# A mixture-of-experts stage regrouped: 20 tiles of four 32-token blocks in place of 24 tiles of two 64-token blocks

## The chip, the cores and the metric

The kernel runs on one core of one Trainium2 chip. The metric is the device time of one execution in microseconds (us), of which the profile covers the span from the first to the last instruction. A core has TensorE (PE; its weight loads are shown as PEld), VectorE (DVE), ScalarE (ACT), GpSimd (POOL) and SyncE (SP), each with its own instruction stream. They meet at semaphores. An engine name with a q behind it is that engine's sequencer, which runs register and branch instructions and hands the others to the engine.

## The reference

16 sequences of 128 tokens with 192 features go through an embedding stage, one attention block and a Switch mixture of 16 experts:

```python
h = tok_embeddings(...)                                  # gathers, time features, layer norm
h = h + attention(_layernorm(h), ...)                    # 12 heads of 16
...
probs = softmax(normed @ w_router); expert_idx = argmax(probs)
keep = onehot * (cumsum(onehot, axis=1) <= 64)           # at most 64 tokens per sequence and expert
expert_in = einsum('bsec,bsd->becd', dispatch, normed)
hidden = relu(einsum('becd,edf->becf', expert_in, wi))   # 192 -> 768
expert_out = einsum('becf,efd->becd', hidden, wo)        # 768 -> 192
h = h + (x + router_prob * where(routed, combined, normed))
```

So each token meets one expert's `wi` (192x768) and `wo` (768x192), in float32.

## The kernel before

The kernel does embeddings and attention for eight pairs of sequences, stores one row per token to DRAM, and writes each token's number into the list of its expert. Then comes the expert stage, which is what the change is about.

Each expert's list is cut into blocks of `BT` = 64 tokens, the last one padded. With 2048 tokens and 16 experts that can be 48 blocks, so the stage always runs `NTILE` = 24 tiles of two blocks. Which expert a block belongs to depends on the data: VectorE works it out in 21 small steps, the plan (`planned(...)`, L1158 to L1213), which leaves in `blk_col` the column at which each block's expert begins in the big `weights` tile. All 16 experts are kept there; they are loaded during the attention stage by SP's queue, the last of them under conditions written out in that queue (L341 to L349).

Per tile q, five engines work in a chain of semaphores, each in the order of its own code:

- GpSimd fetches the tile's 128 token numbers (`list_tile`, L507), then the 128 rows (`gather_rows`, L515, up to three tiles ahead), and at the end scatters the results (`scatter`, L522).
- VectorE reads the two blocks' columns from `blk_col` into registers (`columns`, L1189, one `value_load` for each block), copies both experts' `wi` and later `wo` from there into `w_now` (`take_weights`, L1185, each copy 128x1152), because TensorE cannot address by a register here. `w_now` has two buffers. It also scales and adds the output (`result`, L1195 for the index, L1199 for the rows).
- TensorE transposes the rows (L1459, L1460), multiplies by `wi` (`hidden`, L1467 with 128 rows of the array, L1472 with 64), transposes the hidden layer (L1479) and multiplies by `wo` (`output`, L1488). The two blocks use the two column halves of the array side by side.
- ScalarE copies the transposed rows (L708), applies relu (L712) and copies the transposed hidden layer (L716).

TensorE's order is `turn_rows(q+1)`, `turn_hid(q)`, `hidden(q+1)`, `output(q)`. VectorE's order in the loop is

```python
for q in range(NTILE):
    if q + 1 < NTILE:
        at = columns(q + 1)
        take_weights(q + 1, 0)
    if q >= 1:
        result(q - 1)
    if q + 1 < NTILE:
        take_weights(q + 1, 1)
```

`take_weights(q, part)` waits until the tile that last used the buffer is through (`b_hid` after the hidden matmuls, `b_y` after the output matmuls): with two buffers that is tile q-2.

Of the kernel before, what the change touches and what calls it, by code (L numbers as in the profile page):

```python
# [17 lines left out]
ALU = mybir.AluOpType  # L18
# [16 lines left out]
SLOTS = NSEQ * CAP  # L35
BT = P // 2
SPLIT = SLOTS // BT
# [12 lines left out]

NBLK = NSEQ * P // BT + NE
NTILE = NBLK // 2
ROW = 2 * D + 1
# [13 lines left out]
def tower_kernel(nc, t, out):  # L67
    assert NBLK == 48 and NTILE == 24
    ctx = ExitStack()
    with ctx:  # L70
# [62 lines left out]
        rank_a, rank_b, rank_c = (share_a(8 * NE).rearrange("p (n e) -> p n e", e=NE) for _ in range(3))  # L133
        chosen = share_a(2 * P)[:, 0:8 * NE // 2].bitcast(BF16).rearrange("p (n e) -> p n e", e=NE)
# [133 lines left out]
        LG = 0  # L268
        RANK_STEPS = 12

        block = ctx.enter_context(nc.Block())
# [3 lines left out]
        def _(sp):  # L275
# [81 lines left out]
        def _(pool):  # L357
# [18 lines left out]
                           allow_small_or_imprecise_dtypes=True).then_inc(sem("ident"), 1)  # L376
            nc.gpsimd.iota(blk_idx[:, :], [[2, NTILE]], base=0, channel_multiplier=0,
                           allow_small_or_imprecise_dtypes=True).then_inc(sem("ident"), 1)
# [73 lines left out]
            def enlist(n):  # L452

                if n == 0:
                    pool.wait_ge(sem("lists0"), 16)
                    pool.wait_ge(sem("halves"), 4)
# [89 lines left out]
        def _(act):  # L546
# [179 lines left out]
            act.wait_ge(sem("rows_last"), 32)  # L726
            act.wait_ge(sem("out_last"), 32)
            turn_rows(0)
# [10 lines left out]
        def _(dve):  # L739
# [79 lines left out]
            def constants():  # L819
                dve.wait_ge(sem("vectors"), 16)  # L820
                dve.wait_ge(sem("ident"), 8)
                V.tensor_scalar(low_half[:, :], token_iota[:, 0:1], float(BT), None, ALU.is_ge).then_inc(sem("halves"), 1)
                dve.wait_ge(sem("halves"), 1)
# [322 lines left out]
            dve.wait_ge(sem("bases"), NSEQ + 1)  # L1146
            dve.wait_ge(sem("halves"), 4)
# [4 lines left out]
            over_k = shared[:, 5632:5632 + NE * SPLIT].rearrange("p (e k) -> p e k", k=SPLIT)  # L1152

# [22 lines left out]

            def take_weights(q, part):
# [4 lines left out]
                for e in range(max(2 * q, ARENA_FIRST), min(2 * q + 2, NE)):  # L1182
                    dve.wait_ge(sem(f"weights{e}"), 80)
                for k in range(2):
                    V.tensor_copy(w_now[q % 2][k][:, lo:hi], weights[:, bass.ds(at[k] + lo, hi - lo)]).then_inc(  # L1185
                        sem(("wi_now", "wo_now")[part]), 1)
# [16 lines left out]
            dve.wait_ge(sem("weights"), 80 * ARENA_FIRST)  # L1203
            at = columns(0)
            take_weights(0, 0)
            planned(V.tensor_tensor(big, over(expert_iota[:, :]), ej.unsqueeze(2).broadcast_to([P, NTILE, NE]), ALU.is_equal))
# [6 lines left out]
            planned(V.tensor_scalar(blk_pen[:, :], within, BIG, None, ALU.mult))  # L1213
            take_weights(0, 1)
# [12 lines left out]
        def _(pe):  # L1227
# [234 lines left out]
            def hidden(q):  # L1462
                pe.wait_ge(sem("gT"), q + 1)
                pe.wait_ge(sem("wi_now"), 2 * q + 2)
                for b in range(2):
                    for k in range(2):
                        T.matmul(hid_ps[k * BT:(k + 1) * BT, b, :], gT[:, b * P + k * BT:b * P + (k + 1) * BT],  # L1467
                                 w_now[q % 2][k][:, b * WI2:(b + 1) * WI2], start=True, stop=False)
                for b in range(2):
                    for k in range(2):  # L1470
                        at = (1 - b) * P + k * BT
                        last = T.matmul(hid_ps[k * BT:(k + 1) * BT, b, :], gT[REST[b], at:at + BT],  # L1472
                                        w_now[q % 2][k][REST[b], FF:WI_COLS], start=False, stop=True)
                last.then_inc(sem("b_hid"), 1)
# [7 lines left out]
            def output(q):  # L1482
                pe.wait_ge(sem("hidT"), q + 1)
                pe.wait_ge(sem("wo_now"), 2 * q + 2)
                freed(pe, sem("res"), q - 1)
                for c in range(FC):
                    for k in range(2):
                        last = T.matmul(psum[q % 2][k * BT:(k + 1) * BT, 3, 0:D], hidT[:, c * P + k * BT:c * P + (k + 1) * BT],  # L1488
                                        w_now[q % 2][k][:, WI_COLS + c * D:WI_COLS + (c + 1) * D], start=c == 0, stop=c == FC - 1)
                last.then_inc(sem("b_y"), 1)  # L1490
# [64 lines left out]
```

## Time and profile before

| | |
|---|---|
| median of 3 runs | 388.18 us (387.72 to 389.49) |
| the profiled execution's own time | 388.62 us |
| its span | 386.9 us |
| TensorE busy | 337.5 us, 87% |
| VectorE busy | 258.0 us, 67% |
| ScalarE busy | 160.9 us, 42% |
| GpSimd busy | 198.4 us, 51% |
| mean granted TensorE clock | 0.901 of full speed |

The profile is of one execution. 1.7 us of its time lie outside the span. Busy time counts an engine's own instructions, not those of its sequencer, so time in which a sequencer reads a register shows only as a gap that is put down to "issue". The shares are means over the embedding, attention and expert stages; the expert stage lies from about 236 us to the end.

### The profile page before, as it was taken

What the parts mean: (1) busy time and instruction counts of PE and PEld (TensorE: products, weight loads), DVE (VectorE), ACT (ScalarE), POOL (GpSimd) and SP (SyncE); (2) the same over time, 40 slices, a digit from 0 to 9 for tenths busy, and PEclk for the clock granted to TensorE, in tenths of its full rate; (3) what the DMA queues carried; (4) which work ended last, traced back from release to release, by engine and by line L of the source; (5) the groups of instructions that cost most, each with busy time, mean ns of one, the idle gap of its engine ahead of it and who ended that gap; (6) DMA issues with size and microseconds to landing.
All of it is one profiled execution on the core that took longest, in us unless ns stands there. A gap on an engine that the chain in (4) does not pass through costs nothing.

```text
span 386.9 us, 8606 instructions
## 1 busy us (share of the span) xinstructions
PE 337.5 (87%) x3170; PEld 217.8 (56%) x3170; DVE 258.0 (67%) x742; ACT 160.9 (42%) x299; POOL 198.4 (51%) x191
## 2 busy tenths in 40 slices
PE   8989679689899999989999724799999999999980
PEld 3435446556677776667777412265556655566550
DVE  7774937864779799996767677745666556655520
ACT  3634334514366665647556320233433334333320
POOL 5776374585268661037101255645765676666421
PEclk9566968955999999999999986899999999999995
DMA  4438921113627873371424390494222211122100
GB/s 91 108 86 224 238 66 44 45 34 50 189 32 160 229 146 90 113 195 55 135 65 122 114 255 0 112 278 129 54 57 54 61 57 35 58 55 60 30 2 0
DMA packets 35066, 37.96 MB, mean 98 GB/s; under 512 B 6214, under 2 KB 32531, under 8 KB 35022
## 3 DMA queue, kind: packets, MB, share of 16 engines
q1 hardware_dynamic: 25680, 24.20, 21.7%
q0 software_dynamic: 8768, 12.63, 15.0%
q10 hardware_dynamic: 576, 0.59, 0.5%
q8 instruction: 25, 0.41, 0.4%
q14 instruction: 17, 0.14, 0.1%
HBM read 30.97 MB, written 7.21 MB: 99 GB/s over the span
## 4 chain that ended last, share of the span: by engine, by line
PE 60%; DVE 20%; issue 7%; POOL 4%; ACT 3%; DMA 2%; POOLq 0%; DVEq 0%; ACTq 0%
PE psum L1488 13%; PE psum L1467 9%; PE psum L1238 6%; PE psum L1239 5%; PE psum L1472 5%; PE psum L1479 4%; PE psum L1294 4%; PE psum L1308 4%; POOL weights L392 2%; DVE small L835 2%; PE psum L1459 2%; PE psum L1374 2%; PE psum L1232 1%; DMA weights<-pair_rows,ids 1%; DVE weights L794 1%
## 5 line engine op out<-in xcount | busy, mean ns | idle before, releaser
L1185 DVE COPY shared<-weights 128x1152 f32 x96 | 69.7, 769 | 10.9 <-issue 10.2
L522 POOL DMA_INDIRECT tower_out<-shared,oidx x24 | 36.2, 1507 | 37.3 <-DVE shared L1199 34.7
L1488 PE MATMUL psum<-shared 128*64 128x192 f32 x576 | 52.1, 330 | 0.9 <-ACT shared L716 0.9
L1488 PEld LDWEIGHTS psum<-shared 128*64 128x64 f32 x576 | 39.2, 137 | 19.4 <-issue 13.8
L1199 DVE SCALAR_TENSOR_TENSOR shared<-psum,shared 128x192 f32<-128x192 f32 x24 | 10.0, 418 | 47.1 <-PE psum L1488 47.1
L1467 PE MATMUL psum<-shared 128*64 128x384 f32 x192 | 36.8, 505 | 0.5 <-ACT shared L708 0.5
L1238 PE MATMUL psum<-shared,weights 96*128 96x192 f32 (+1 forms) x96 | 36.0, 460 | 0.7 <-ACT weights L574 0.7
L916 DVE TENSOR_REDUCE guard<-psum 128x12 bf16<-128x1536 f32 x16 | 28.1, 1754 | 10.9 <-PE psum L1294 10.9
L712 ACT ACTIVATE shared<-psum 128x768 f32<-128x768 f32 x24 | 19.5, 812 | 37.6 <-PE psum L1472 37.6
L431 POOL TENSOR_TENSOR small<-small,mhalf 128x2 f32<-128x2 f32 x16 | 12.3, 771 | 44.1 <-DVE small L843 44.0
L1239 PE MATMUL psum<-shared,weights 97*128 97x192 f32 (+1 forms) x96 | 33.0, 428 | 0.0
L515 POOL DMA_INDIRECT shared<-token_rows,blk_token x24 | 26.1, 1086 | 11.0 <-issue 6.4
L708 ACT COPY shared<-psum 128x256 f32<-128x256 f32 x24 | 8.9, 372 | 52.6 <-PE psum L1460 52.6
L507 POOL DMA_INDIRECT blk_token<-expert_lists,blk_entry x24 | 23.7, 990 | 9.8 <-issue 7.0
L450 POOL TENSOR_TENSOR small<-small,mhalf 128x4 f32<-128x4 f32 x8 | 8.7, 1084 | 37.7 <-DVE small L955 37.7
L458 POOL DMA_INDIRECT expert_lists<-tokens,slot_i x16 | 15.8, 987 | 18.6 <-DVE slot_i L1042 14.5
L608 ACT ACTIVATE shared<-psum 128x1536 f32<-128x1536 f32 x16 | 23.2, 1448 | 3.7 <-PE psum L1317 3.6
L1239 PEld LDWEIGHTS psum<-shared,weights 97*128 97x128 f32 x96 | 19.8, 215 | 6.0 <-issue 3.0
L716 ACT COPY shared<-psum 128x768 f32<-128x768 f32 x24 | 19.2, 800 | 9.0 <-PE psum L1479 9.0
L880 DVE TENSOR_REDUCE ms_qk<-weights 128x24 f32<-128x408 f32 x16 | 9.2, 577 | 20.5 <-ACT weights L579 20.5
L579 ACT ACTIVATE weights<-psum 128x384 f32<-128x384 f32 x16 | 7.9, 491 | 34.7 <-PE psum L1239 34.7
L1472 PE MATMUL psum<-shared 64*64 64x384 f32 x192 | 21.7, 523 | 0.0
(196 smaller groups left out, 714.8 us busy)
## 6 DMA issues: line engine op xcount, KB each, us to landing
weights<-in_wo SPq DMA_DIRECT2D x16, 576.0 KB, 6.9
weights<-in_wi SPq DMA_DIRECT2D x32, 192.0 KB, 4.8
weights<-in_wi SPq DMA_DIRECT2D x32, 96.0 KB, 5.2
token_rows<-shared SPq DMA_DIRECT2D x14, 192.5 KB
tower_out<-shared SPq DMA_DIRECT2D x14, 96.0 KB
token_rows<-shared ACTq DMA_DIRECT2D x2, 192.5 KB, 3.0
blk_token<-expert_lists,blk_entry POOLq DMA_INDIRECT x24, 2.5
shared<-token_rows,blk_token POOLq DMA_INDIRECT x24, 3.3
```

Source lines behind the costliest of these rows:

```text
L507: G.indirect_dma_start(out=blk_token[:, q:q + 1], out_offset=None, in_=lists, in_offset=bass.IndirectOffsetOnAxis(ap=blk_entry[:, q:q + 1] ...
L515: G.indirect_dma_start(out=grow[q % 4], out_offset=None, in_=rows, in_offset=bass.IndirectOffsetOnAxis(ap=blk_token[:, q:q + 1], axis=0),) ...
L522: G.indirect_dma_start(out=out, out_offset=bass.IndirectOffsetOnAxis(ap=oidx[q % 2][:, :], axis=0), in_=res[q % 2], in_offset=None, bounds ...
L608: S.activation(probsT[u], psum_s.rearrange("p b c -> p (b c)"), ACT.Exp).then_inc(sem(f"probs{u}"), 1)
L712: S.activation(hid.rearrange("p (b c) -> p b c", b=2), hid_ps, ACT.Relu).then_inc(sem("hid"), 1)
L916: V.tensor_reduce(guard16[u][:, :].rearrange("p (g c) -> p g c", c=HPAD)[:, :, 0:CHUNKS], psum_s.rearrange("p g (c m) -> p g c m", m=P), A ...
L1185: V.tensor_copy(w_now[q % 2][k][:, lo:hi], weights[:, bass.ds(at[k] + lo, hi - lo)]).then_inc(sem(("wi_now", "wo_now")[part]), 1)
L1238: T.matmul(dst, xt[0:HALF, 0:P], w[0:HALF, 0, start:start + width], start=True, stop=False)
L1239: return T.matmul(dst, xt[0:k1, P:2 * P], w[0:k1, 1, start:start + width], start=False, stop=True)
L1467: T.matmul(hid_ps[k * BT:(k + 1) * BT, b, :], gT[:, b * P + k * BT:b * P + (k + 1) * BT], w_now[q % 2][k][:, b * WI2:(b + 1) * WI2], start ...
L1472: last = T.matmul(hid_ps[k * BT:(k + 1) * BT, b, :], gT[REST[b], at:at + BT], w_now[q % 2][k][REST[b], FF:WI_COLS], start=False, stop=True)
L1488: last = T.matmul(psum[q % 2][k * BT:(k + 1) * BT, 3, 0:D], hidT[:, c * P + k * BT:c * P + (k + 1) * BT], w_now[q % 2][k][:, WI_COLS + c * ...
```

## The change

Blocks have 32 tokens instead of 64 (`NB` = 4, `BT` = 32). That makes at most 80 blocks, in 20 tiles of four; a tile still has 128 tokens. The four blocks use the four column quarters of the array. Four experts' weights fill the room that the two buffers of two had, so `w_now` has one buffer: the copies for tile q wait for `hidden(q-1)` and `output(q-1)`. VectorE copies three of the four experts and reads three columns; ScalarE copies the fourth and reads its column (`take_last`, `last_column`), and for the first tile it waits for the end of the whole plan. In VectorE's loop the copies of `wo` for tile q come after those of `wi` for tile q+1, and `result(q-1)` comes last. In SP's queue expert 12 is loaded together with 10 and 11, and the last two no longer wait for the row gather of tile 2 (`rows2`). The plan's arrays and two constants are sized anew.

```diff
-BT = P // 2
+NB = 4
+BT = P // NB
...
-        w_now = [[share_b(WCOL) for _ in range(2)] for _ in range(2)]
+        w_now = [share_b(WCOL) for _ in range(NB)]
...
-            for e in (10, 11):
+            for e in (10, 11, 12):
                 load_expert(e)
             sp.wait_ge(sem("p_logit0"), NPAIR)
             sp.wait_ge(sem("p_logit1"), NPAIR)
-            sp.wait_ge(sem("rows2"), 16)
-            for e in (12, NE - 2, NE - 1):
-                load_expert(e)
+            load_expert(NE - 2)
+            load_expert(NE - 1)
...
+            def take_last(q, part):
+                lo, hi = ((0, WI_COLS), (WI_COLS, WCOL))[part]
+                freed(act, sem(("b_hid", "b_y")[part]), q)
...
+                S.copy(w_now[NB - 1][:, lo:hi], weights[:, bass.ds(last_at[q % 2] + lo, hi - lo)]).then_inc(
+                    sem(("wi_last", "wo_last")[part]), 1)
...
+            act.wait_ge(sem("plan"), N_PLAN)
+            last_at = [last_column(0), None]
+            take_last(0, 0)
+            take_last(0, 1)
             turn_rows(0)
             relu(0)
             for q in range(NTILE):
                 if q + 1 < NTILE:
+                    last_at[(q + 1) % 2] = last_column(q + 1)
+                    take_last(q + 1, 0)
                     turn_rows(q + 1)
                 turn_hid(q)
+                if q >= 1:
+                    take_last(q, 1)
                 if q + 1 < NTILE:
                     relu(q + 1)
...
-                if q >= 2:
-                    dve.wait_ge(sem(("b_hid", "b_y")[part]), q - 1)
+                freed(dve, sem(("b_hid", "b_y")[part]), q)
...
-                return [dve.value_load(blk_col[k * BT:k * BT + 1, q:q + 1], min_val=0, max_val=(NE - 1) * WCOL) for k in range(2)]
+                return [dve.value_load(blk_col[k * BT:k * BT + 1, q:q + 1], min_val=0, max_val=(NE - 1) * WCOL) for k in range(NB - 1)]
...
             for q in range(NTILE):
                 if q + 1 < NTILE:
-                    at = columns(q + 1)
-                    take_weights(q + 1, 0)
+                    at[(q + 1) % 2] = columns(q + 1)
+                    take_weights(q + 1, 0, (0, 1, 2))
                 if q >= 1:
+                    take_weights(q, 1, (0, 1, 2))
                     result(q - 1)
-                if q + 1 < NTILE:
-                    take_weights(q + 1, 1)
             result(NTILE - 1)
```

What this does to the order is seen best in VectorE's stream. Before, one tile in the middle of the stage reads as follows (L1195 and L1199 are `result`, TENSOR_LOAD with its two ISA rows is one `value_load`, a COPY with the ISA row ahead of it is one copy of weights; the piece ends with the first of two `wi` copies):

```order
L1195 TENSOR_TENSOR oidx<-blk_token,blk_pen 128x1 [waits s_scattered1,s_blk_token1]
L1199 SCALAR_TENSOR_TENSOR shared<-psum,shared 128x192 [waits s_oidx,s_b_y]
L1185 ISA [waits s_b_y]
L1185 COPY shared<-weights 128x1152
L1185 ISA
L1185 COPY shared<-weights 128x1152
L1189 TENSOR_LOAD blk_col
L1189 ISA x2
L1189 TENSOR_LOAD blk_col
L1189 ISA x2
L1185 ISA [waits s_b_hid]
L1185 COPY shared<-weights 128x1152
```

Of the changed kernel the same stretch of VectorE's stream, from `result` (now L1221 and L1225) to the first of three `wi` copies (L1211):

```order
L1221 TENSOR_TENSOR oidx<-blk_token,blk_pen 128x1 [waits s_scattered1,s_blk_token1]
L1225 SCALAR_TENSOR_TENSOR shared<-psum,shared 128x192 [waits s_oidx,s_b_y]
L1215 TENSOR_LOAD blk_col
L1215 ISA x2
L1215 TENSOR_LOAD blk_col
L1215 ISA x2
L1215 TENSOR_LOAD blk_col
L1215 ISA x2
L1211 ISA [waits s_b_hid]
L1211 COPY shared<-weights 128x1152
```

The two `wo` copies that stood between `result` and the register loads are gone from there; three loads follow the row instruction at once, and all six copies follow the loads.

On ScalarE the entry into the stage read, before (row copy and relu of tile 0, then row copy, hidden copy and relu of the loop):

```order
L708 COPY shared<-psum 128x256 [waits s_b_gT,s_out_last,s_rows_last]
L712 ACTIVATE shared<-psum 128x768 [waits s_b_hid]
L708 COPY shared<-psum 128x256 [waits s_b_gT]
L716 COPY shared<-psum 128x768 [waits s_b_hidT]
L712 ACTIVATE shared<-psum 128x768 [waits s_b_hid]
```

and in the changed kernel (L740 is `last_column`, L736 the copy of weights, L710, L714 and L718 what L708, L712 and L716 were):

```order
L740 TENSOR_LOAD blk_col [waits s_weights,s_blk_entry,s_plan,s_out_last,s_rows_last]
L740 ISA x2
L736 ISA
L736 COPY shared<-weights 128x1152
L736 ISA
L736 COPY shared<-weights 128x1152
L710 COPY shared<-psum 128x256 [waits s_b_gT]
L714 ACTIVATE shared<-psum 128x768 [waits s_b_hid]
L740 TENSOR_LOAD blk_col
L740 ISA x2
L736 ISA [waits s_b_hid]
L736 COPY shared<-weights 128x1152
```

A load and two copies, behind the plan's end, now stand ahead of the row copy of tile 0; in the loop a load and a copy stand between relu and the next row copy.

## Rows read from the trace of the kernel before

**Rows 1.** Busy time of each engine in three stretches, with granted clock and DMA.

```profile
core 0: us, PE busy (x) PEld busy (x) DVE busy (x) ACT busy (x) POOL busy (x), PEclk, DMA share, GB/s
...
215.00:220.00 5.00, 3.68 (x39) 2.06 (x40) 3.88 (x17) 1.16 (x3) 0.00 (x0) 1.00 0.37 123
225.00:230.00 5.00, 0.71 (x7) 0.54 (x6) 3.59 (x21) 1.67 (x6) 3.23 (x4) 0.83 0.97 269
270.00:370.00 100.00, 100.00 (x894) 58.86 (x888) 60.94 (x112) 36.89 (x56) 65.38 (x54) 1.00 0.19 50
```

**Rows 2.** TensorE in order of time, one tile of the steady stage.

```profile
302.77 0.82 PE L1479 MATMUL psum<-ident,shared 128*128 128x128 f32 x6
303.52 1.51 PE L1467 MATMUL psum<-shared 128*64 128x384 f32 x8
...
305.77 2.17 PE L1488 MATMUL psum<-shared 128*64 128x192 f32 x24
307.87 0.33 PE L1459 MATMUL psum<-ident,shared 128*128 128x128 f32 x1
```

**Rows 3.** VectorE in order of time, the same tile.

```profile
302.62 0.42 DVE L1199 SCALAR_TENSOR_TENSOR shared<-psum,shared 128x192 f32<-128x192 f32 x1 [1.80 <-PE psum L1488]
302.95 1.42 DVE L1185 COPY shared<-weights 128x1152 f32 x2
304.71 1.44 DVE L1185 COPY shared<-weights 128x1152 f32 x2 [0.34 <-issue]
306.07 0.14 DVE L1195 TENSOR_TENSOR oidx<-blk_token,blk_pen 128x1 int32<-128x1 int32 x1
307.99 0.42 DVE L1199 SCALAR_TENSOR_TENSOR shared<-psum,shared 128x192 f32<-128x192 f32 x1 [1.78 <-PE psum L1488]
```

**Rows 4.** Instructions of line 1189 on VectorE's sequencer, 302 to 306.3 us.

```profile
L1189 DVEq TENSOR_LOAD <-blk_col x2: 528/529/530, 302.9 to 303.7; - x2
L1189 DVEq FUSED_REGOPS  x2: 190/190/190, 303.5 to 304.3; - x2
```

**Rows 5.** TensorE in order of time, a matmul of the attention stage on column quarters.

```profile
135.23 0.86 PE L1334 MATMUL psum<-shared,weights 128*32 128x128 f32 x24
```

**Rows 6.** GpSimd in order of time, a scatter of the steady stage.

```profile
303.87 1.72 POOL L522 DMA_INDIRECT tower_out<-shared,oidx  x1 [1.03 <-DVE shared L1199]
```

**Rows 7.** All engines in order of time, entry into the expert stage.

```profile
236.29 0.18 DVE L1175 TENSOR_TENSOR blk_entry<-shared 128x24 int32<-128x24 f32 x1
...
238.37 1.43 DVE L1185 COPY shared<-weights 128x1152 f32 x2 [1.90 <-issue]
...
240.30 0.95 POOL L515 DMA_INDIRECT shared<-token_rows,blk_token  x1 [0.32 <-issue]
...
242.78 1.55 DVE L1185 COPY shared<-weights 128x1152 f32 x2 [0.16 <-DVE blk_pen L1213]
...
244.51 2.07 PE L1467 MATMUL psum<-shared 128*64 128x384 f32 x8 [0.54 <-ACT shared L708]
...
248.00 0.47 PE L1459 MATMUL psum<-ident,shared 128*128 128x128 f32 x1
```

**Rows 8.** ScalarE's groups of instructions, busy us and mean ns, whole span.

```profile
L608 ACT ACTIVATE shared<-psum 128x1536 f32<-128x1536 f32 x16 | 23.2, 1448 | 3.7 <-PE psum L1317 3.6
...
L716 ACT COPY shared<-psum 128x768 f32<-128x768 f32 x24 | 19.2, 800 | 9.0 <-PE psum L1479 9.0
...
L708 ACT COPY shared<-psum 128x256 f32<-128x256 f32 x24 | 8.9, 372 | 52.6 <-PE psum L1460 52.6
```

**Rows 9.** SP's queue in order of time, the last load of expert 11.

```profile
224.06 0.59 SPq L304 DMA_DIRECT2D weights<-in_wo  x1
```

**Rows 10.** DMA issues with median us to landing, 236 to 240 us.

```profile
blk_token<-expert_lists,blk_entry POOLq DMA_INDIRECT x2, 2.5
```

**Rows 11.** The same view, 250 to 262 us.

```profile
blk_token<-expert_lists,blk_entry POOLq DMA_INDIRECT x1, 5.9
```

**Rows 12.** All engines in order of time, the end of the kernel.

```profile
376.31 0.42 DVE L1199 SCALAR_TENSOR_TENSOR shared<-psum,shared 128x192 f32<-128x192 f32 x1 [3.38 <-PE psum L1488]
377.53 0.97 POOL L522 DMA_INDIRECT tower_out<-shared,oidx  x1 [2.89 <-DVE shared L1199]
```

More of the change, by code:

```diff
@@ L51 @@
 NBLK = NSEQ * P // BT + NE
-NTILE = NBLK // 2
+NTILE = NBLK // NB
 ROW = 2 * D + 1
@@ L67, in tower_kernel @@
 def tower_kernel(nc, t, out):
-    assert NBLK == 48 and NTILE == 24
+    assert NBLK == 80 and NTILE == 20
     ctx = ExitStack()
@@ L132, in tower_kernel @@
         bases = share_a(NSEQ * NE).rearrange("p (n e) -> p n e", e=NE)
-        rank_a, rank_b, rank_c = (share_a(8 * NE).rearrange("p (n e) -> p n e", e=NE) for _ in range(3))
+        rank_a = share_a(8 * NE).rearrange("p (n e) -> p n e", e=NE)
+        rank_b = share_a(8 * SPLIT).rearrange("p (n k) -> p n k", k=SPLIT)
         chosen = share_a(2 * P)[:, 0:8 * NE // 2].bitcast(BF16).rearrange("p (n e) -> p n e", e=NE)
@@ L269, in tower_kernel @@
         RANK_STEPS = 12
+        N_PLAN = 21
         block = ctx.enter_context(nc.Block())
@@ L376, in _ @@
                            allow_small_or_imprecise_dtypes=True).then_inc(sem("ident"), 1)
-            nc.gpsimd.iota(blk_idx[:, :], [[2, NTILE]], base=0, channel_multiplier=0,
+            nc.gpsimd.iota(blk_idx[:, :], [[NB, NTILE]], base=0, channel_multiplier=0,
                            allow_small_or_imprecise_dtypes=True).then_inc(sem("ident"), 1)
@@ L455, in enlist @@
                     pool.wait_ge(sem("lists0"), 16)
-                    pool.wait_ge(sem("halves"), 4)
+                    pool.wait_ge(sem("halves"), 6)
                 pool.wait_ge(sem("slots"), batch_of(n) + 1)
@@ L727, in _, with last_column @@
             act.wait_ge(sem("out_last"), 32)
+            def take_last(q, part):
+                lo, hi = ((0, WI_COLS), (WI_COLS, WCOL))[part]
+                freed(act, sem(("b_hid", "b_y")[part]), q)
+                for e in range(max(NB * q, ARENA_FIRST), min(NB * q + NB, NE)):
+                    act.wait_ge(sem(f"weights{e}"), 80)
+                S.copy(w_now[NB - 1][:, lo:hi], weights[:, bass.ds(last_at[q % 2] + lo, hi - lo)]).then_inc(
+                    sem(("wi_last", "wo_last")[part]), 1)
+            def last_column(q):
+                return act.value_load(blk_col[(NB - 1) * BT:(NB - 1) * BT + 1, q:q + 1], min_val=0, max_val=(NE - 1) * WCOL)
+            act.wait_ge(sem("blk_entry"), 1)
+            act.wait_ge(sem("weights"), 80 * ARENA_FIRST)
+            act.wait_ge(sem("plan"), N_PLAN)
+            last_at = [last_column(0), None]
+            take_last(0, 0)
+            take_last(0, 1)
             turn_rows(0)
@@ L822, in constants @@
                 V.tensor_scalar(low_half[:, :], token_iota[:, 0:1], float(BT), None, ALU.is_ge).then_inc(sem("halves"), 1)
-                dve.wait_ge(sem("halves"), 1)
+                for k in range(1, NB - 1):
+                    dve.wait_ge(sem("halves"), k)
+                    V.scalar_tensor_tensor(low_half[:, :], token_iota[:, 0:1], float((k + 1) * BT), low_half[:, :], ALU.is_ge, ALU.add).then_inc(sem("halves"), 1)
+                dve.wait_ge(sem("halves"), NB - 1)
                 V.scalar_tensor_tensor(half_pos[:, :], low_half[:, :], -float(BT), token_iota[:, 0:1], ALU.mult, ALU.add).then_inc(sem("halves"), 1)
@@ L1146, in _ @@
             dve.wait_ge(sem("bases"), NSEQ + 1)
-            dve.wait_ge(sem("halves"), 4)
+            dve.wait_ge(sem("halves"), 6)
             big, big2 = (shared[:, 4608 + 512 * k:4608 + 512 * k + NTILE * NE].rearrange("p (j e) -> p j e", e=NE) for k in range(2))
@@ L1151, in _ @@
             nth, ej, before, within, length, late = (cols(plan, 112 + 32 * a, NTILE) for a in range(6))
-            over_k = shared[:, 5632:5632 + NE * SPLIT].rearrange("p (e k) -> p e k", k=SPLIT)
+            over_k = shared[:, 6288:6288 + NE * SPLIT].rearrange("p (e k) -> p e k", k=SPLIT)
             def over(v):
@@ L1175, in _, with take_weights @@
             V.tensor_tensor(blk_entry[:, :], length, late, ALU.add).then_inc(sem("blk_entry"), 1)
-            def take_weights(q, part):
+            def take_weights(q, part, blocks):
                 lo, hi = ((0, WI_COLS), (WI_COLS, WCOL))[part]
-                if q >= 2:
-                    dve.wait_ge(sem(("b_hid", "b_y")[part]), q - 1)
-                for e in range(max(2 * q, ARENA_FIRST), min(2 * q + 2, NE)):
+                freed(dve, sem(("b_hid", "b_y")[part]), q)
+                for e in range(max(NB * q, ARENA_FIRST), min(NB * q + NB, NE)):
                     dve.wait_ge(sem(f"weights{e}"), 80)
-                for k in range(2):
-                    V.tensor_copy(w_now[q % 2][k][:, lo:hi], weights[:, bass.ds(at[k] + lo, hi - lo)]).then_inc(
+                for k in blocks:
+                    V.tensor_copy(w_now[k][:, lo:hi], weights[:, bass.ds(at[q % 2][k] + lo, hi - lo)]).then_inc(
                         sem(("wi_now", "wo_now")[part]), 1)
             def columns(q):
-                return [dve.value_load(blk_col[k * BT:k * BT + 1, q:q + 1], min_val=0, max_val=(NE - 1) * WCOL) for k in range(2)]
+                return [dve.value_load(blk_col[k * BT:k * BT + 1, q:q + 1], min_val=0, max_val=(NE - 1) * WCOL) for k in range(NB - 1)]
             def result(q):
@@ L1203, in _ @@
             dve.wait_ge(sem("weights"), 80 * ARENA_FIRST)
-            at = columns(0)
-            take_weights(0, 0)
+            at = [columns(0), None]
+            take_weights(0, 0, (0, 1))
             planned(V.tensor_tensor(big, over(expert_iota[:, :]), ej.unsqueeze(2).broadcast_to([P, NTILE, NE]), ALU.is_equal))
@@ L1213, in _ @@
             planned(V.tensor_scalar(blk_pen[:, :], within, BIG, None, ALU.mult))
-            take_weights(0, 1)
+            assert steps[0] == N_PLAN
+            take_weights(0, 0, (2,))
+            take_weights(0, 1, (0, 1, 2))
             for q in range(NTILE):
                 if q + 1 < NTILE:
-                    at = columns(q + 1)
-                    take_weights(q + 1, 0)
+                    at[(q + 1) % 2] = columns(q + 1)
+                    take_weights(q + 1, 0, (0, 1, 2))
                 if q >= 1:
+                    take_weights(q, 1, (0, 1, 2))
                     result(q - 1)
-                if q + 1 < NTILE:
-                    take_weights(q + 1, 1)
             result(NTILE - 1)
@@ L1463, in hidden @@
                 pe.wait_ge(sem("gT"), q + 1)
-                pe.wait_ge(sem("wi_now"), 2 * q + 2)
+                pe.wait_ge(sem("wi_now"), (NB - 1) * (q + 1))
+                pe.wait_ge(sem("wi_last"), q + 1)
                 for b in range(2):
-                    for k in range(2):
+                    for k in range(NB):
                         T.matmul(hid_ps[k * BT:(k + 1) * BT, b, :], gT[:, b * P + k * BT:b * P + (k + 1) * BT],
-                                 w_now[q % 2][k][:, b * WI2:(b + 1) * WI2], start=True, stop=False)
+                                 w_now[k][:, b * WI2:(b + 1) * WI2], start=True, stop=False)
                 for b in range(2):
-                    for k in range(2):
+                    for k in range(NB):
                         at = (1 - b) * P + k * BT
                         last = T.matmul(hid_ps[k * BT:(k + 1) * BT, b, :], gT[REST[b], at:at + BT],
-                                        w_now[q % 2][k][REST[b], FF:WI_COLS], start=False, stop=True)
+                                        w_now[k][REST[b], FF:WI_COLS], start=False, stop=True)
                 last.then_inc(sem("b_hid"), 1)
@@ L1483, in output @@
                 pe.wait_ge(sem("hidT"), q + 1)
-                pe.wait_ge(sem("wo_now"), 2 * q + 2)
+                pe.wait_ge(sem("wo_now"), (NB - 1) * (q + 1))
+                pe.wait_ge(sem("wo_last"), q + 1)
                 freed(pe, sem("res"), q - 1)
                 for c in range(FC):
-                    for k in range(2):
+                    for k in range(NB):
                         last = T.matmul(psum[q % 2][k * BT:(k + 1) * BT, 3, 0:D], hidT[:, c * P + k * BT:c * P + (k + 1) * BT],
-                                        w_now[q % 2][k][:, WI_COLS + c * D:WI_COLS + (c + 1) * D], start=c == 0, stop=c == FC - 1)
+                                        w_now[k][:, WI_COLS + c * D:WI_COLS + (c + 1) * D], start=c == 0, stop=c == FC - 1)
                 last.then_inc(sem("b_y"), 1)
```

## The prediction

> **What bounds the kernel now.** I went first to the stage that the change touches and read the busy time of each engine in it. From 270 to 370 us TensorE is busy all the time at full clock, VectorE and GpSimd some 60 to 65%, ScalarE 37% [rows 1]. Then TensorE in order of time: one group follows the other with no gap, 0.75 of hidden transposes (302.77 to 303.52), 2.25 of hidden matmuls (to 305.77), 2.10 of output matmuls (to 307.87), where the next tile's row transposes begin [rows 2]. VectorE's row instructions lie 307.99 - 302.62 = 5.37 apart [rows 3]; the 0.27 by which that is more than 5.10 are the row transposes. So the 24 tiles run at TensorE's pace, 5.37 us each.
>
> VectorE is the engine that gets more work, so its slack has to be read with care, and busy time isn't enough. Two copies take 1.42, then there is a gap of 0.34 put down to issue, then the other two, then 1.78 of waiting for TensorE [rows 3]. The gap is the end of something longer. VectorE's sequencer reads two block columns from 302.9 on: 0.53 for a load, 0.19 for the register work, 0.8 from one load to the next [rows 4], and the copy that needs them starts at 304.71. The two reads take 1.8 us, of which 1.47 lie hidden under the two copies that were handed to the engine just before.
>
> **TensorE's new work.** 20 tiles in place of 24 at an unchanged tile would take off 4 x 5.37 = 21.5 us. Each output or hidden matmul becomes two of half the columns of the array with the same moving width. Four quarters side by side do occur before: 24 instructions of 128 columns in about 0.8 us [rows 5], 3.9 columns per ns, against 24 of 192 in 2.10, 2.2 per ns, on halves [rows 2]. Twice the instructions at that rate make the output 2.36 and the other 128-row matmuls 1.58 instead of 1.44. The 64-row matmuls on quarters have no row: between no loss (0.8 a tile) and half the width lost (1.6), and I take no loss, since the same groups of 64 rows work side by side now (2.25 less 1.51 [rows 2] leaves them about half of what the 128-row ones take). So TensorE's own tile is 5.4 to 6.6 us.
>
> **VectorE's new tile.** Here is the step on which I rest the forecast. With one buffer and three experts a tile has six copies and three reads. In the new order the row instruction waits for the index instruction of the same engine, which waits behind all six copies; the sequencer stops at that wait, so it reaches the reads only when the engine has run dry. Then only the 0.42 of the row instruction covers them, no copies. The cycle, from one row instruction to the next:
> - row instruction to first read: 0.1 (between 0.05 and the 0.28 from 302.62 to 302.9, which had two copies to hand out);
> - three reads up to the first copy: 1.81 for two (302.9 to 304.71), plus 0.8: 2.6 [rows 3, 4];
> - six copies: 3 x 1.42 less two overlaps of 0.08 (306.15 - 306.07): 4.10 [rows 3];
> - the index instruction's 0.14 less its overlap, 0.06, and the wait on it, 0.1 (0.05 to 0.15).
>
> That is 6.96 us. Copies and GpSimd get in each other's way: a scatter beside copies took 1.72 [rows 6], one beside an idle VectorE 0.97 [rows 12], and a pair of copies beside a gather 1.55 instead of 1.42 [rows 7]. From 0 to 3 x 0.13 a tile; in the steady stage the copies lost nearly nothing, so I take 0.14. A tile takes 7.1 us (6.9 to 7.35). That is above TensorE's 5.4 to 6.6, so VectorE sets the pace and TensorE waits for `wi` at every tile. With its copies starting at T, `wi` is there at T+2.2, hidden is done at T+4.45, output at T+6.55, and VectorE needs none of these sooner: it waits for nobody.
>
> The Trainium skill (DMA: Bandwidth & Descriptors, Latency and other measured facts) puts a floor of about 600 ns under a tensor_load. The row shows 0.53, and the row decides; by the page's figure three reads would add 0.2 a tile, 3.6 us in all.
>
> **ScalarE** adds two copies of 1152 columns. 1536 cost 1.45 and 768 0.80, so 1152 cost 1.12 [rows 8]. Its tile becomes 2 x 1.12 + 2 x 0.80 + 0.37 = 4.2; its read runs while relu runs. Nothing of it is late at 7.1 a tile. GpSimd, at three issues of about 1 us, each held up by 0.75 at most [rows 6, 12], stays under 7.1 as well (3 x 1.72 = 5.2).
>
> **The entry.** VectorE's plan ends its first part at 236.47; one of its arrays doubles, others shrink by a sixth: 0.3 later (0 to 0.6). Two reads took 1.9 up to 238.37 [rows 7], three take 2.8, so the first copy is at 239.6 and the pair done at 241.0. The eight plan steps behind it took 2.8 (239.8 to 242.6) and now a little less: 243.6. Only then ScalarE starts: a read 1.0, two copies 2.24, the row copy 0.37 [rows 8]. Hidden of tile 0 can't start before 247.4; it started at 244.51 [rows 7].
>
> The other way into tile 0 is list and row gather. Before, SP's queue had given out its last early load at 224.06 [rows 9], and I put the end of that traffic near 231. Now three more experts of 1.18 MB (twice 192 x 768 floats) follow at once; at 269 GB/s [rows 1] they keep it busy for 13 us more, to about 244. Under such loads a list gather landed in 5.9 us instead of 2.5 [rows 10, 11]. The path has three transfers in a row (list write, list gather, row gather), so it is 0 to 8 us later and hidden of tile 0 starts between 247.4 and 252. I take 249, nearer to the lower end, because the last of the three falls behind the loads. The first hidden took 3.5 us (244.51 to 248.00) [rows 7], not 2.25, and I leave it so: done at 252.5. With one buffer only now come relu 0.8, ScalarE's copy 1.12, the row copy 0.37 and 0.2 of gaps: hidden of tile 1 runs from 255.0 to 257.25, and VectorE's copies for tile 2 start at T = 257.25.
>
> **The sum.** From there to the copies for tile 19 are 17 cycles: 17 x 7.1 = 120.7. The end: `wi` 2.2, hidden 2.25, output of tile 18 2.1, transposes 0.75, ScalarE's copy 0.9 and its share of `wo` 1.2, which now waits for output 18, output of tile 19 2.1, 0.1: 11.6. The last row instruction starts at 257.25 + 120.7 + 11.6 = 389.55 instead of 376.31 [rows 12]: 13.2 us later, and what follows is unchanged. The profiled execution's 388.62 become 401.8. The median of the runs is 0.44 lower; on it the sum is 401.4, and I say 401.5. The attention stage is left as it is; its slot steps grow by less than 0.5.
>
> **The rivals.**
> - *Fewer tiles win.* If the reads were reached in time, in the shadow of the copies as now, a VectorE tile would be 4.1 + 0.6 + 0.34 plus contention, about 5.3, and the pace TensorE's, say 5.6. Then 257.25 + 95.2 + 11.6 = 364.05: 12.3 earlier, 376 us. For it speaks that the same reads cost only 0.34 now. Against it: the order rows put them behind the instruction that waits for the engine itself. It decides at 17P = 376.31 - 268.85: below P = 6.32 us a tile the change wins. Chance 0.07, and 0.02 for an end near no change.
> - *TensorE is slower on quarters or cools down.* If nothing ran wider than two, hidden and output would double to 8.7, with the transposes 9.7 a tile: 17 x 2.6 = 44 more, 446 us. And the gaps of 1.7 a tile might lower the clock: it was 0.83 where TensorE was busy 0.71 of 5 us, but full at 3.68 of 5 [rows 1], the share to be expected here. Chance 0.03.
> - *The port.* If GpSimd held a copy up for a whole issue of 0.97 [rows 12] three times a tile, P were 9.9 and the time 449. The copies that ran beside GpSimd lost 0.13, not 0.97 [rows 7]. The Trainium skill (SBUF — State Buffer, SBUF: two separate sides) speaks for this one: it calls the port that the two share an exclusive lock, held for the whole instruction, the other one blocked. The scatter's 1.72 agrees with that for GpSimd; the pair's 1.55 does not for VectorE. Chance 0.03.
> - *The forecast, VectorE at 6.9 to 7.35 a tile*: 0.85.
>
> **The numbers.** The low end takes P = 6.9 (-3.4) and hidden at 247.4 (-1.6): 396.5. The high end takes P = 7.35 (+4.3) and hidden at 252 (+3): 409. The cases outside hold about 2 in 10. A measurement of this kernel can tell about 0.5%, 1.9 us, from no change; faster 0.07, same 0.02, slower 0.91.
>
> **What the new profile would show.** VectorE's row instruction every 7.1 us, then a gap of 2.2 put down to issue, then six copies without a gap; TensorE waiting about 1.7 a tile before its hidden matmuls, for VectorE's copy; hidden of tile 0 at about 249. If the distance is 5.6 and TensorE has no gaps, the reads were hidden and I am wrong in sign. If TensorE's matmuls take longer than 5.4 in sum, the quarters cost. If the gap ahead of the copies is 2.2 but copies are longer, it is the port.

## The result, and the profile after

The changed kernel took 398.32 us (median of 4 runs, 394.63 to 399.23), the kernel before 387.95 us beside it (4 runs, 386.11 to 389.49). The ratio is 1.0251, 95% interval 1.0171 to 1.0331 (the ratios here and below are not quotients of the medians and differ from them by up to 0.003). The profiled execution took 399.23 us with a span of 397.5; before it was 388.62 and 386.9.

VectorE in order of time, one tile of the steady stage of the changed kernel (start, duration, then what it is, and in brackets the idle time before it):

```profile
310.47 0.42 DVE L1225 SCALAR_TENSOR_TENSOR shared<-psum,shared 128x192 f32<-128x192 f32 x1
312.90 4.23 DVE L1211 COPY shared<-weights 128x1152 f32 x6 [2.02 <-issue]
317.05 0.15 DVE L1221 TENSOR_TENSOR oidx<-blk_token,blk_pen 128x1 int32<-128x1 int32 x1
317.30 0.42 DVE L1225 SCALAR_TENSOR_TENSOR shared<-psum,shared 128x192 f32<-128x192 f32 x1
```

This answers to [rows 3]. The row instructions lie 317.30 - 310.47 = 6.83 apart, where it was 5.37. In this stretch VectorE never waits for TensorE any more: the 1.78 in front of the row instruction is gone. The one gap in the cycle is 2.02 in front of the six copies, put down to "issue", where a gap of 0.34 was.

TensorE in order of time, the same tile and on to the next tile's first transpose:

```profile
315.18 1.50 PE L1495 MATMUL psum<-shared 128*32 128x384 f32 x16 [1.42 <-issue]
316.61 0.88 PE L1500 MATMUL psum<-shared 64*32 64x384 f32 x16
317.41 2.16 PE L1517 MATMUL psum<-shared 128*32 128x192 f32 x48
319.50 0.33 PE L1486 MATMUL psum<-ident,shared 128*128 128x128 f32 x1
```

Hidden takes 317.41 - 315.18 = 2.23 and output 319.50 - 317.41 = 2.09. Before it was 2.25 and 2.10 [rows 2], with half the instructions. Ahead of the hidden matmuls TensorE now stands still for 1.42 a tile. The label says "issue", but VectorE's copies say what it is: the first three of six, at 0.7 each, are through at about 312.90 + 2.1 = 315.0, and the matmuls begin at 315.18. ScalarE's copy of the fourth expert, from 311.46 on for 1.14, was through long before, at 312.60.

The register reads, line 1215, on VectorE's sequencer (count, shortest/median/longest ns, starts of the first and the last):

```profile
L1215 DVEq TENSOR_LOAD <-blk_col x3: 305/520/524, 317.3 to 318.8; - x3
L1215 DVEq FUSED_REGOPS  x3: 183/190/190, 317.9 to 319.3; - x3
```

And the wait ahead of the row instruction, line 1223, on the same sequencer (317 to 317.5 us):

```profile
L1223 DVEq EVENT_SEMAPHORE  x1: 21/21/21, 317.2 to 317.2; - x1
```

This is the wait for the index instruction, which ends at 317.05 + 0.15 = 317.2. It stands on the sequencer itself, and in this tile nothing that comes after it in VectorE's stream starts earlier. The first of the three loads starts at the same time as the row instruction, 317.3, and the last one's register work ends at 319.5. That is what fills the "issue" gap. Busy time of each engine in a stretch of the stage, with granted clock:

```profile
280.00:370.00 90.00, 70.40 (x1144) 38.99 (x1144) 61.68 (x106) 53.47 (x67) 45.83 (x40) 1.00 0.16 43
```

TensorE has gone from 100% [rows 1] to 78%, and VectorE, which sets the pace, shows only 69%: a sequencer's reads aren't in its busy time. The chain around the entry and the end, all engines in order of time:

```profile
240.86 1.39 POOL L509 DMA_INDIRECT blk_token<-expert_lists,blk_entry  x1 [5.61 <-DMA expert_lists<-tokens,slot_i]
...
244.91 2.21 ACT L736 COPY shared<-weights 128x1152 f32 x2 [16.80 <-DVE blk_pen L1239]
...
248.53 0.33 PE L1486 MATMUL psum<-ident,shared 128*128 128x128 f32 x1 [2.14 <-DMA shared<-token_rows,blk_token]
...
249.46 2.79 PE L1495 MATMUL psum<-shared 128*32 128x384 f32 x16 [0.46 <-ACT shared L710]
...
258.04 4.16 DVE L1211 COPY shared<-weights 128x1152 f32 x6 [2.61 <-PE psum L1500]
...
374.97 4.10 DVE L1211 COPY shared<-weights 128x1152 f32 x6 [2.01 <-issue]
...
384.51 3.32 PE L1517 MATMUL psum<-shared 128*32 128x192 f32 x48 [2.14 <-DVE shared L1225]
...
387.87 0.42 DVE L1225 SCALAR_TENSOR_TENSOR shared<-psum,shared 128x192 f32<-128x192 f32 x1 [3.39 <-PE psum L1517]
```

Hidden of tile 0 starts at 249.46, where it was 244.51 [rows 7]. The copies for tile 2 start at 258.04 and those for tile 19 at 374.97, so 17 cycles take 116.93, 6.88 each. The last row instruction starts at 387.87, which is 11.56 later than before [rows 12].

### The profile page after: what moved, and what is told of

Read it like the earlier page. It is cut to its first block, busy times and chain, and to the rows that moved or that the text cites. A ratio compares the mean times of both kernels' runs of the same rounds, so it can differ in the third digit from the quotient of the medians.

```text
span 397.5 us, 10011 instructions
## 1 busy us (share of the span) xinstructions
PE 318.0 (80%) x3766; PEld 202.7 (51%) x3778; DVE 273.4 (69%) x760; ACT 195.0 (49%) x327; POOL 180.5 (45%) x179
## 4 chain that ended last, share of the span: by engine, by line
PE 53%; DVE 20%; issue 13%; DMA 5%; POOL 4%; ACT 3%; DVEq 1%; POOLq 0%; ACTq 0%
PE psum L1517 11%; PE psum L1495 8%; PE psum L1265 6%; PE psum L1266 5%; PE psum L1500 4%; PE psum L1321 4%; PE psum L1335 3%; PE psum L1507 3%; POOL weights L394 2%; DMA expert_lists<-tokens,slot_i 2%; DVE small L862 2%; DMA weights<-pair_rows,ids 1%; PE psum L1401 1%; PE psum L1259 1%; PE psum L1486 1%
## 5 line engine op out<-in xcount | busy, mean ns | idle before, releaser
L1211 DVE COPY shared<-weights 128x1152 f32 x120 | 84.2, 768 | 48.9 <-issue 37.8
L736 ACT COPY shared<-weights 128x1152 f32 x40 | 45.9, 1151 | 16.9 <-DVE blk_pen L1239 16.8
L1495 PE MATMUL psum<-shared 128*32 128x384 f32 x320 | 31.2, 508 | 25.3 <-issue 24.2
L524 POOL DMA_INDIRECT tower_out<-shared,oidx x20 | 20.3, 1015 | 67.2 <-DVE shared L1225 63.8
L1517 PE MATMUL psum<-shared 128*32 128x192 f32 x960 | 44.3, 334 | 2.1 <-DVE shared L1225 2.1
L1517 PEld LDWEIGHTS psum<-shared 128*32 128x32 f32 x960 | 30.2, 112 | 20.6 <-issue 14.2
L714 ACT ACTIVATE shared<-psum 128x768 f32<-128x768 f32 x20 | 16.2, 810 | 39.3 <-PE psum L1500 39.3
L1495 PEld LDWEIGHTS psum<-shared 128*32 128x32 f32 x320 | 10.0, 111 | 36.8 <-issue 35.0
L509 POOL DMA_INDIRECT blk_token<-expert_lists,blk_entry x20 | 21.9, 1094 | 11.4 <-issue 5.8
L1321 PE MATMUL psum<-weights 32*128 32x128 f32 x384 | 20.5, 302 | 1.2 <-ACT weights L593 1.0
L1321 PEld LDWEIGHTS psum<-weights 32*128 32x128 f32 x384 | 17.4, 203 | 7.2 <-issue 4.8
```

Of the source, the lines that this page charges most:

```text
L509: G.indirect_dma_start(out=blk_token[:, q:q + 1], out_offset=None, in_=lists, in_offset=bass.IndirectOffsetOnAxis(ap=blk_entry[:, q:q + 1] ...
L524: G.indirect_dma_start(out=out, out_offset=bass.IndirectOffsetOnAxis(ap=oidx[q % 2][:, :], axis=0), in_=res[q % 2], in_offset=None, bounds ...
L736: S.copy(w_now[NB - 1][:, lo:hi], weights[:, bass.ds(last_at[q % 2] + lo, hi - lo)]).then_inc(sem(("wi_last", "wo_last")[part]), 1)
L1211: V.tensor_copy(w_now[k][:, lo:hi], weights[:, bass.ds(at[q % 2][k] + lo, hi - lo)]).then_inc(sem(("wi_now", "wo_now")[part]), 1)
L1321: last = T.matmul(psum_s[:, g, c * P:(c + 1) * P], qT[u][rows_, c * P:(c + 1) * P], kT[u][rows_, c * P:(c + 1) * P], start=True, stop=True)
```

## The experiments

The theory was that the three reads stand bare behind an instruction that waits for its own engine, and that this alone makes each of the 20 tiles longer than TensorE needs; a second, smaller loss is the later entry, from the earlier loads. The rivals were that six copies and single buffering cost this much wherever the reads stand, or that the quarters or the port do.

**reads_early: the changed kernel, with the reads moved.** They stand behind the hand-out of all six copies and ahead of the row instruction, so that the copies cover them. Nothing else is changed.

```diff
             take_weights(0, 1, (0, 1, 2))
+            at[1] = columns(1)
             for q in range(NTILE):
                 if q + 1 < NTILE:
-                    at[(q + 1) % 2] = columns(q + 1)
                     take_weights(q + 1, 0, (0, 1, 2))
                 if q >= 1:
                     take_weights(q, 1, (0, 1, 2))
+                if q + 2 < NTILE:
+                    at[q % 2] = columns(q + 2)
+                if q >= 1:
                     result(q - 1)
```

Expected: 

> The changed kernel with VectorE's three register reads moved up: they stand behind the hand-out of the six copies and ahead of result, so that they run while the copies run; nothing else is changed. Theory (the reads behind result's wait set the pace): the gap of 2.0 us ahead of the copies goes, VectorE needs about 4.8 us a tile, TensorE sets the pace again at 5.4 to 5.5, and 17 cycles x 1.4 us less than 6.83 give about 24 us: 374 to 377 us, faster than both kernels. Rival (the single buffer's waits, or the width of the matmuls, cost the time): the tile stays above 6.3 us, the time above 388 us.

Measured: 372.46 us (6 runs, 369.87 to 375.82), 0.9595 of the kernel before (0.9568 to 0.9622; 387.58 us beside it). VectorE in order of time: the copies for tile 2, one tile of the steady stage, and the copies for tile 19:

```profile
259.41 4.16 DVE L1211 COPY shared<-weights 128x1152 f32 x6 [2.61 <-PE psum L1503]
...
312.86 0.42 DVE L1225 SCALAR_TENSOR_TENSOR shared<-psum,shared 128x192 f32<-128x192 f32 x1
313.20 4.21 DVE L1211 COPY shared<-weights 128x1152 f32 x6
317.60 0.16 DVE L1221 TENSOR_TENSOR oidx<-blk_token,blk_pen 128x1 int32<-128x1 int32 x1 [0.20 <-issue]
317.87 0.42 DVE L1225 SCALAR_TENSOR_TENSOR shared<-psum,shared 128x192 f32<-128x192 f32 x1
...
350.44 4.22 DVE L1211 COPY shared<-weights 128x1152 f32 x6
```

And the reads on its sequencer, and the engines' busy time in the stage:

```profile
L1215 DVEq TENSOR_LOAD <-blk_col x3: 324/521/525, 315.2 to 316.7; - x3
L1215 DVEq FUSED_REGOPS  x3: 183/190/190, 315.8 to 317.2; - x3
```

```profile
280.00:360.00 80.00, 78.41 (x1302) 43.51 (x1286) 69.68 (x118) 59.71 (x74) 47.60 (x41) 1.00 0.19 53
```

The same three reads take as long as they did, but now they run from 315.2 to 317.4, inside the copies (313.20 to 317.41). The gap of 2.02 is gone. A small one, 0.20, now stands ahead of the index instruction, which comes behind the reads: the reads start only when the hand-out of the `wo` copies is through, and that waits for TensorE's output matmuls, which end at 312.59 + 2.16 = 314.75. Two row instructions here lie 5.01 apart, but that varies from tile to tile; from the copies for tile 2 to those for tile 19 it is 350.44 - 259.41 = 91.03 us for 17 cycles, 5.35 each. TensorE is busy 78.41 of 80 us again and sets the pace. The six copies are still six, the buffer still single, the quarters still quarters. So none of these by itself is what made the tile longer. In the medians the gain is 398.32 - 372.46 = 25.9 us, and 17 cycles give 116.93 - 91.03 = 25.9. The profiled execution, the slowest of the six at 375.82 us, gained 23.4 on the changed kernel's: its cycles began 1.4 us later, and the rest lies behind them.

**read_extra: one more read.** The reverse test: VectorE reads a fourth column, whose value nothing uses.

```diff
-                return [dve.value_load(blk_col[k * BT:k * BT + 1, q:q + 1], min_val=0, max_val=(NE - 1) * WCOL) for k in range(NB - 1)]
+                return [dve.value_load(blk_col[k * BT:k * BT + 1, q:q + 1], min_val=0, max_val=(NE - 1) * WCOL) for k in range(NB)]
```

Expected: 

> The changed kernel with a fourth register read per tile on VectorE, whose value nobody uses. Theory: each read adds its 0.8 us to each of some 18 tiles, so the tile goes from 6.83 to 7.65 us and the time by 14 us to about 413 us. Rival (the copies or the single buffer set the pace and the reads lie in a wait): less than 3 us more.

Measured: 408.06 us (4 runs, 406.84 to 409.18), 1.0528 of before (1.0495 to 1.0562), 9.7 us over the changed kernel. VectorE in order of time, and the reads on its sequencer:

```profile
312.45 0.42 DVE L1225 SCALAR_TENSOR_TENSOR shared<-psum,shared 128x192 f32<-128x192 f32 x1
315.50 4.16 DVE L1211 COPY shared<-weights 128x1152 f32 x6 [2.63 <-issue]
...
319.83 0.42 DVE L1225 SCALAR_TENSOR_TENSOR shared<-psum,shared 128x192 f32<-128x192 f32 x1
```

```profile
L1215 DVEq TENSOR_LOAD <-blk_col x4: 306/413/524, 312.5 to 314.8; - x4
```

The cycle is 7.38, the gap 2.63. The direction is as expected, since nothing covers a read here; the size is not. I had counted 0.8 for a read, and it cost 2.63 - 2.02 = 0.61; the time rose by 9.7 us instead of 14. The loads' median of 413 ns between 306 and 524 says that two of the four took the short time, two the long one.

**before_loads_early: the queue alone.** The kernel before, with only SP's queue of the changed kernel.

```diff
-            for e in (10, 11):
+            for e in (10, 11, 12):
                 load_expert(e)
             sp.wait_ge(sem("p_logit0"), NPAIR)
             sp.wait_ge(sem("p_logit1"), NPAIR)
-            sp.wait_ge(sem("rows2"), 16)
-            for e in (12, NE - 2, NE - 1):
-                load_expert(e)
+            load_expert(NE - 2)
+            load_expert(NE - 1)
```

Expected: 

> The kernel before with only SP's queue changed: expert 12 with 10 and 11, the last two without the wait for the row gather of tile 2. Theory: list and row gather of tile 0 land about 5 us later, hidden of tile 0 starts at about 249 instead of 244.5 and nothing later gives it back: 392 to 393 us. Rival: the transfers are hidden, 388 us.

Measured: 393.69 us (4 runs, 391.37 to 396.5), 1.0128 of before (1.0083 to 1.0174). All engines in order of time at its entry:

```profile
248.60 0.48 PE L1458 MATMUL psum<-ident,shared 128*128 128x128 f32 x1 [2.62 <-DMA shared<-token_rows,blk_token]
...
249.83 0.91 PE L1466 MATMUL psum<-shared 128*64 128x384 f32 x2 [0.54 <-ACT shared L707]
```

The first transpose waits for the row gather, and hidden of tile 0 starts at 249.83 instead of 244.51 [rows 7], with VectorE's and ScalarE's code untouched. So three experts loaded ahead of the gathers delay the entry by about 5 us by themselves. In the medians the kernel is 6.1 us slower, a little more than expected.

**loads_late: the queue undone.** The changed kernel, with SP's queue of the kernel before (the diff above, reversed).

Expected: 

> The changed kernel with SP's queue as it was before: experts 12, 14 and 15 are loaded behind the row gather of tile 2. Theory (the loads brought forward delay list and row gather at the entry): hidden of tile 0 starts at about 247.5 us instead of 249.5, held by ScalarE's two copies behind the plan, and the time falls by 2 us to about 396 us, with the same 6.83 us a tile. Rival (the loads cost nothing, or the late ones hold up tile 3): no change or slower.

Measured: 397.71 us (4 runs, 397.06 to 398.4), 1.0258 of before (1.0231 to 1.0285), which is no measurable difference to the changed kernel. All engines in order of time, entry and tile 3:

```profile
243.43 2.21 ACT L737 COPY shared<-weights 128x1152 f32 x2 [16.92 <-DVE blk_pen L1240]
...
245.96 2.79 PE L1496 MATMUL psum<-shared 128*32 128x384 f32 x16 [2.63 <-ACT shared L711]
...
264.07 2.10 DVE L1212 COPY shared<-weights 128x1152 f32 x3 [4.60 <-DMA weights<-in_wo]
```

Hidden of tile 0 is early again, 245.96 instead of 249.46. Not all of these 3.5 us come from the loads: in this profile the plan itself ended 1.5 us earlier than in the changed kernel's (242.48 against 243.96). But the last experts now land so late that the copies for tile 3 wait 4.60 us for them. The copies for tile 2 start at 254.71, 3.3 us earlier than in the changed kernel; those for tile 3 start at 264.07, and there it was 265.01. Four experts a tile means that the last weights are wanted sooner than before: most of the entry's gain comes back as a wait for weights. It is the second half of the rival, the late loads that hold up tile 3, that came true, and not the 396 us of the theory.

**reads_early_loads_late: reads moved, queue undone, and ScalarE freed from the plan's end.** The reads stand as in reads_early; the rest of the edit is

```diff
-            for e in (10, 11, 12):
+            for e in (10, 11):
                 load_expert(e)
...
-            load_expert(NE - 2)
-            load_expert(NE - 1)
+            sp.wait_ge(sem("rows2"), 16)
+            for e in (12, NE - 2, NE - 1):
+                load_expert(e)
...
-            act.wait_ge(sem("plan"), N_PLAN)
```

Expected: 

> The same as reads_early_loads_mid, but with the loads where they were in the kernel before, behind the row gather of tile 2. Theory (what loads_late gained at the entry it gave back where tile 3 waited for expert 15, until 264 us): hidden of tile 0 starts at about 245 us, the copies of tile 3 wait for the loads until about 264, some 5 us, and the time is that of reads_early, 371 to 373 us. Rival (the loads are not what tile 3 waited for): like reads_early_loads_mid.

Measured: 377.6 us (4 runs, 375.1 to 379.13), 0.9726 of before (0.9665 to 0.9787; 388.94 us beside it). VectorE in order of time, the copies for tile 3:

```profile
266.33 2.10 DVE L1211 COPY shared<-weights 128x1152 f32 x3 [8.15 <-DMA weights<-in_wo]
```

With the shorter cycle the copies for tile 3 are wanted sooner still, and the wait grows to 8.15. The mechanism was expected, its size was not: I had put the wait at some 5 us, 3 too low, and the time at 371 to 373.

**reads_early_loads_mid: the same, but the three experts wait for the row gather of tile 0 (`rows0`), not of tile 2.** Against the kernel just described:

```diff
-            sp.wait_ge(sem("rows2"), 16)
+            sp.wait_ge(sem("rows0"), 16)
```

Expected: 

> reads_early with two changes at the entry: experts 12, 14 and 15 are loaded when the rows of tile 0 have landed (neither at once, as in the changed kernel, nor after tile 2's, as before), and ScalarE's copies for tile 0 wait for the part of the plan that ends with the list entries, not for all of it. Theory (two causes hold up the entry: the loads beside list and row gather, and ScalarE behind the whole plan; the reads are gone already): hidden of tile 0 starts at about 245 us, the loads end at about 257 and are there for tile 3, whose copies start at about 259; 4 to 5 us less than reads_early, 367 to 369 us. Rival (the loads hold up tile 3 as in loads_late, or the later gathers): no better than 372 us.

Measured: 370.82 us (6 runs, 367.07 to 372.01), 0.9536 of before (0.9485 to 0.9587; 388.94 us beside it). TensorE and VectorE in order of time:

```profile
245.69 2.79 PE L1498 MATMUL psum<-shared 128*32 128x384 f32 x16 [0.46 <-ACT shared L711]
...
262.02 4.16 DVE L1211 COPY shared<-weights 128x1152 f32 x6 [2.40 <-DMA weights<-in_wo]
```

Hidden of tile 0 starts at 245.69, as expected. But 2.40 us of waiting for weights are left, the copies for tile 3 start at 262.02 and not at 259, and the time misses the expected 367 to 369. The interval overlaps that of reads_early, so that it is better than that one isn't shown. Both beat the kernel before.

## Why the prediction was right

**VectorE's cycle, the step on which the forecast rests.** Its mechanism holds: the reads start with the row instruction, find an empty engine, and end ahead of the first copy; moving them takes the loss away, adding one makes it larger. Its terms: up to the first copy 312.90 - 310.47 = 2.43, for which the prediction had 0.1 + 2.6; copies, index instruction and wait 317.30 - 312.90 = 4.40, for which it had 4.10 + 0.06 + 0.1 and 0.14 of contention, the same 4.40. So the cycle came out at 6.83 here and 6.88 over the stage instead of 7.1, and 17 x 0.22 = 3.7 us of the sum were too much. The term that was mis-sized is the three reads: it was built from two loads of 0.53, but of the three loads in the changed kernel one takes 0.31, which is the 0.22. That the sequencer stops at the wait is shown by the wait itself, at 317.2, and the first load right behind it.

**TensorE's work on quarters.** For the 64-row matmuls the value for no loss was the right one. The two other terms were put too high, 2.36 for the output and 1.58 for the 128-row matmuls: it is 2.09 and 316.61 - 315.18 = 1.43. With 2.23 + 2.09 a tile against 4.35 before, the quarters cost nothing. VectorE set the pace, so that error had no part in the sum. The bound of half the width lost for 64 rows (1.6) is out: the 16 instructions take 0.8. The same two numbers rule out the rival of slower quarters. Its other half, a cooler TensorE, shows behind the entry only in the last output: see the end, below. The granted clock was 1.00 from 280 to 370 us, with TensorE busy 70.40 of 90.

**The entry.** Forecast for hidden of tile 0 was 249, between 247.4 and 252; it was 249.46. The lower bound's reason, ScalarE behind the whole plan, was there: its two copies end at 244.91 + 2.21 = 247.12, and a row copy of 0.37 behind them makes 247.5. But it didn't end last. The row gather landed at 248.53, where the first transpose begins. It came behind a list gather for which GpSimd had waited 5.61 us for the list write; it started at 240.86, and before at 237.25, when VectorE's plan released it:

```profile
237.25 0.99 POOL L507 DMA_INDIRECT blk_token<-expert_lists,blk_entry  x1 [2.83 <-DVE blk_entry L1175]
```

That is the loads: they make 249.83 in the kernel before, where ScalarE copies no weights, and without them hidden starts at 245.96, right behind ScalarE's copies and under the bound by 1.4, since the plan ended 1.5 earlier there. T came at 258.04 instead of 257.25.

**The end.** From T + 17 cycles to the last row instruction it took 387.87 - 374.97 = 12.9 instead of 11.6. Most of the difference is the last output: 3.32 us instead of 2.1. The wait ahead of it was in the forecast, as ScalarE's copy and its share of `wo`; VectorE and ScalarE in order of time:

```profile
381.73 2.10 DVE L1211 COPY shared<-weights 128x1152 f32 x3 [2.07 <-PE psum L1517]
382.40 0.80 ACT L718 COPY shared<-psum 128x768 f32<-128x768 f32 x1 [2.02 <-PE psum L1507]
383.10 1.16 ACT L736 COPY shared<-weights 128x1152 f32 x1
```

The view puts the wait ahead of the last output down to VectorE's row instruction. By the code that output waits for both engines' `wo` copies and not for the row instruction of tile 18: VectorE's are through at 383.83, ScalarE's at 384.26, and the output starts at 384.51. TensorE's busy time and granted clock of the changed kernel in the last two stretches show why the output took longer:

```profile
382.00:384.50 2.50, 0.36 (x4) 0.15 (x3) 2.38 (x6) 1.85 (x2) 0.00 (x0) 1.00 0.08 27
384.50:388.00 3.50, 3.32 (x48) 2.39 (x48) 0.13 (x1) 0.00 (x0) 0.97 (x1) 0.62 0.02 4
```

TensorE waits 2.14 us, in the end for ScalarE's copy, and the 48 instructions behind that wait run at a mean granted clock of 0.62, between the two levels (1.2 and 2.4 GHz are 0.5 and 1.0) and nearer the lower. The prediction left the lower clock out. Behind the last row instruction, 397.5 - 387.87 = 9.6 us of span are left, where it was 386.9 - 376.31 = 10.6, so what was put as unchanged was 1.0 shorter.

**The sum.** Predicted were 13.2 us more on the profiled execution; it is 399.23 - 388.62 = 10.6: 0.8 for T, -3.7 for the cycles, 1.3 for the end and -1.0 behind it add up to -2.6. Their signs differ, so part of the closeness is luck: the cycles alone would have put the forecast 3.7 too high. The median of the changed kernel is 3.2 below the forecast.

**The rivals.** That fewer tiles win was worked out at 376 us if the reads stayed covered. They don't in the changed kernel, and reads_early, in which they do, takes 372.46 with a cycle of 5.35 (the prediction had 5.6). So this rival's price was sound to about 4 us, and only its condition was not met. For the port, the copies would have had to stretch. GpSimd in order of time beside the six copies of 312.90 in the changed kernel:

```profile
313.02 1.47 POOL L517 DMA_INDIRECT shared<-token_rows,blk_token  x1 [0.30 <-issue]
314.80 1.08 POOL L509 DMA_INDIRECT blk_token<-expert_lists,blk_entry  x1 [0.30 <-issue]
```

With these two issues beside them the six copies took 4.23; the six at 374.97, behind GpSimd's last gather, took 4.10. So the two issues cost VectorE 0.13, about the 0.14 that was put for it, and GpSimd's gather took 1.47. The exclusive lock of the Trainium skill (SBUF — State Buffer, SBUF: two separate sides) doesn't show on VectorE's side at that size: two whole issues would have been 1.47 + 1.08 = 2.55 us.

**What stays open.** Why a read takes 0.31 us one time and 0.52 another was not tried. Nor was the reason given for the weight copies, that TensorE cannot address by a register: in both kernels its matmuls read `w_now` at fixed places, and no run here tries it otherwise.

## What to carry to other kernels

A register read on an engine's sequencer doesn't count as busy. Here three of them were free while the engine still had copies that were handed to it, and cost 2.0 us a tile where it had none. So place reads behind the hand-out of long instructions and ahead of the first wait for the engine itself. Where an engine that sets the pace looks only 70% busy, look at its sequencer for the gaps put down to "issue". And when a transfer is moved, ask who wants the moved data first: here a load moved later freed the entry and stalled tile 3.

## What the runs showed of the hardware that was not expected

- Of three register loads in a row the second took 0.31 us and the others 0.52; of four, by their median of 413 ns, two took the short time. Where the second of two was read before, both took 0.53 [rows 4].
- Four 32-column quarters cost TensorE nothing against two 64-column halves: 48 instructions of 192 columns in 2.09 us, 24 of them in 2.10 before [rows 2].
- A wait of 2.14 us at the end, with TensorE busy 0.36 of 2.50 us, was followed by a mean granted clock of 0.62, while 70.40 of 90 us in the stage, with a gap of 1.4 in every tile, went on at 1.00.
